# V' of a cross-attention block through device memory: all of it in fp32r rows, and context columns in another order

## The reference, cut to what matters

```
qh = layernorm(x) @ Wq ; kh = ctx @ Wk ; vh = ctx @ Wv        (16 heads of 64)
attn = softmax(causal(qh kh^T / 8))
x = x + concat_heads(attn vh) @ Wo + bo
h = layernorm(x); x = x + bitlinear(silu(bitlinear(h, w_gate)) * bitlinear(h, w_up), w_down)
```

## Time and profile before

| what | value |
|---|---|
| median of 3 runs | 697.3 us (696.67 to 698.23) |
| the profiled execution's own time | 696.44 us |
| its span, first to last instruction | 694.6 us |
| PE busy | 670.0 us, 96% of the span |
| DVE, ACT, POOL busy | 538.7, 488.2, 350.1 us |
| DMA | 63.04 MB moved, 91 GB/s over the span |
| mean granted PE clock, 1 being full speed | 0.990 |

### The profile page before, as it was taken

One profiled execution on the slowest core, in us unless ns is written; L12 is line 12 of the kernel. 1 busy time (PEld: TensorE's weight loads), 2 busy tenths in 40 slices (PEclk: granted clock), 3 DMA queues, 4 the chain that ended last, 5 costly groups with the idle time before them and its releaser, 6 DMA issues.

```text
span 694.6 us, 18984 instructions
## 1 busy us (share of the span) xinstructions
PE 670.0 (96%) x7235; PEld 450.7 (65%) x7266; DVE 538.7 (78%) x1398; ACT 488.2 (70%) x864; POOL 350.1 (50%) x357
## 2 busy tenths in 40 slices
PE   8999999999999999999999999999999999999963
PEld 5576766677666667666666767666676766667451
DVE  5667878777788777787877778787777887787976
ACT  5768767767866767876676787667678667768543
POOL 0536554554555555455455455546454554644541
PEclk9999999999999999999999999999999999999995
DMA  8023433333433434343333334343333433332421
GB/s 267 2 77 92 99 86 85 86 96 88 109 100 74 95 77 102 84 115 78 97 88 82 103 86 110 81 92 86 85 100 92 110 74 96 86 82 72 99 60 38
DMA packets 71834, 63.04 MB, mean 91 GB/s; under 512 B 43584, under 2 KB 47936, under 8 KB 71744
## 3 DMA queue, kind: packets, MB, share of 16 engines
q1 hardware_dynamic: 71744, 61.83, 36.4%
HBM read 15.91 MB, written 4.19 MB: 29 GB/s over the span
## 4 chain that ended last, share of the span: by engine, by line
PE 91%; DVE 3%; issue 2%; POOL 2%; DMA 1%; ACT 0%; POOLq 0%; SPq 0%; DVEq 0%
PE ps_up L460 8%; PE ps_up L344 7%; PE ps_a L485 7%; PE ps_b L571 6%; PE ps_up L333 5%; PE ps_up L334 4%; PE ps_up L335 4%; PE ps_kv L344 4%; PE ps_low L344 4%; PE ps_a L489 4%; PE ps_low L470 4%; PE ps_u L553 2%; PE ps_up L352 2%; PE ps_up L354 2%; PE ps_up L353 2%
## 5 line engine op out<-in xcount | busy, mean ns | idle before, releaser
L665 ACT ACTIVATE vp<-ps_up 128x512 f32<-128x512 f32 x61 | 36.4, 597 | 134.5 <-PE ps_up L344 134.5
L1192 POOL TENSOR_TENSOR prob_up<-prob_up,row_rec 128x512 f32<-128x512 f32 x62 | 63.8, 1051 | 125.3 <-DVE row_rec L975 125.3
L1178 POOL TENSOR_TENSOR hid_b<-hid,neg_round 128x512 bf16<-128x512 f32 x62 | 63.1, 1039 | 94.8 <-ACT hid L665 94.8
L1183 POOL TENSOR_TENSOR prob_up<-prob_up,row_max 128x1024 f32<-128x1024 f32 x31 | 59.3, 1913 | 61.0 <-DVE row_max L960 61.0
L1024 DVE SCALAR_TENSOR_TENSOR gated<-gated,ps_g 128x512 f32<-128x512 f32 x60 | 41.2, 687 | 54.3 <-ACT gated L749 53.3
L953 DVE SCALAR_TENSOR_TENSOR prob_up<-ps_up,rs,bias_up 128x512 f32<-128x512 f32 x62 | 43.7, 747 | 45.3 <-PE ps_up L460 45.3
L665 ACT ACTIVATE kp<-ps_up 128x512 f32<-128x512 f32 x124 | 71.0, 605 | 10.1 <-PE ps_up L335 7.5
L485 PEld LDWEIGHTS ps_a<-vp,prob_t 128*32 128x32 f32 x1984 | 55.3, 110 | 19.0 <-issue 17.9
L460 PE MATMUL ps_up<-kp,xt 128*32 128x256 f32 (+1 forms) x768 | 61.9, 454 | 0.0
L344 PE MATMUL ps_up<-n_w,ct 128*32 128x512 f32 x504 | 60.2, 593 | 0.9 <-DVE prob_up L953 0.9
L485 PE MATMUL ps_a<-vp,prob_t 128*32 128x128 f32 x1984 | 59.9, 273 | 0.8 <-ACT prob_t L665 0.8
(11 more groups left out here) (257 smaller groups left out, 1806.5 us busy)
## 6 DMA issues: line engine op xcount, KB each, us to landing
vp<-v_rows SPq DMA_DIRECT2D x496, 64.0 KB, 2.0
ct<-in_ctx_t SPq DMA_DIRECT2D x16, 256.0 KB, 2.9
x_res<-in_x SPq DMA_DIRECT2D x16, 256.0 KB, 2.8
xt<-in_x_t SPq DMA_DIRECT2D x16, 256.0 KB, 3.2
out<-x SPq DMA_DIRECT2D x32, 128.0 KB, 2.4
kp<-v_rows SPq DMA_DIRECT2D x16, 64.0 KB, 2.0
hid_t<-hid_b SPq DMA_TRANSPOSE x62, 2.9
kp<-in_wk SPq DMA_DIRECT2D x2, 256.0 KB, 4.0
```

The costliest lines, as they stand in the source:

```text
L665: copy = lambda dst, src, **kw: nc.scalar.activation(dst, src, ACT.Copy, **kw)
L1178: p.tensor_tensor(hid_b[:, c, :], hid[0][:, c, :], neg_round[:].broadcast_to([P, F]), ALU.add).then_inc(hb_ready, 1)
L1183: p.tensor_tensor(up, up, top[:, 0, :].rearrange("p (c h o) -> p c h o", c=1, o=1) .broadcast_to([P, 2, H, R]), ALU.subtract).then_inc(shi ...
L1192: p.tensor_tensor(up[:, half, :, :], up[:, half, :, :], rows(rec[:, 0, :], H, R), ALU.mult).then_inc(normed, 1)
```

## The change

1. **V' wholly by rows.** `v_tiles` is gone. `v_unit` makes eight units for a quad, four for each half (`jh`), each three products as in `v_row_unit`. `v_rows` has eight buffers in place of four. A quad's eight units are made in the period before its own.
2. **Through device memory.** `save_row` writes each unit to a scratch tensor `v_mem` in device memory (4 MB, two quads deep; 256 KB are written per unit); `load_v` reads the quad's whole V' back into `vp` with one 2 MB DMA, or two of 1 MB for the last quad. The 16 moves per quad are gone.
3. **Column order.** The context columns are stored as (half, key, sequence) in place of (half, sequence, key). The K' copies put them back: they read PSUM at a step of four elements and write in order. `sum_ctx` reads at that step too.
4. **Order of the fill.** Between the other work of a period PE places 16 units in the order `o0 o1 o2 o3 k0 k1 o4 k2 o5 k3 o6 k4 o7 k5 k6 k7` (o: V' of the next quad, k: K'), at the positions that the tiles and units had.
5. **N.** ACT writes `n_hi` straight from PSUM, DVE makes `n_lo` from PSUM and `n_hi`; `scores(0)` waits for all four `n_lo`.
6. **Small steps.** POOL makes `rstd2(n-1)` between the upper and the lower subtraction. `sum_ctx` comes after the inverted sums. In the ending several steps of PE, ACT, DVE and POOL change places, and so do PSUM banks.

```diff
-    in_ctx_t: .transpose(0, 5, 1, 3, 2, 4)
+    in_ctx_t: .transpose(0, 5, 1, 3, 4, 2)
-            def v_tiles(n, b, dst):
-                col = (n % 2 * 4 + 2) * P // 2 + b * R
-                for h4 in range(QB):
-                    t = mm(dst[h4 * R:(h4 + 1) * R, :], ct[n // 2 % 2][:, col:col + R], heads_of(n_w, h4), ...)
+            def v_unit(n, u, dst):
+                par, col = n // 2 % 2, (2 * (n % 2) + u // QB) * P
+                cols = slice(col, col + P)
+                hi, lo = heads_of(n_hi, u % QB), heads_of(n_lo, u % QB)
                 mm(dst, ct_hi[par][:, cols], hi, start=True, stop=False)
                 mm(dst, ct_lo[par][:, cols], hi, start=False, stop=False)
                 mm(dst, ct_hi[par][:, cols], lo, start=False, stop=True).then_inc(rows_ready, 1)
-            def move_rows(n, h4):
-                sp.wait_ge(rows_evac, QB * n + h4 + 1)
-                for b in range(QB):
-                    sp.dma_start(vp[...][h4 * R:(h4 + 1) * R, b, 0, :, :], v_rows[h4][b * R:(b + 1) * R, :, :])
+            def save_row(n, u):
+                jh, h4 = u // QB, u % QB
+                if n >= 2:
+                    sp.wait_ge(vp_loaded, 16 * (n - 1))
+                sp.wait_ge(rows_evac, V_UNITS * n + u + 1)
+                sp.dma_start(v_mem[n % 2, h4 * R:(h4 + 1) * R, :, jh, :], v_rows[u][...]).then_inc(rows_saved[u], 16)
+            def load_v(n):
+                if n and n < LAST:
+                    sp.wait_ge(attn_ready, n)
+                for u in range(V_UNITS):
+                    sp.wait_ge(rows_saved[u], 16 * (n + 1))
+                sp.dma_start(vp[last(n)]..., v_mem[n % 2]...).then_inc(vp_loaded, 16)
 SP, per period:  turn_hid(n-2)
-                 move_rows(n, 0..3), load_ctx, load_xt; store(n-2); x_res
+                 load_v(n); x_res; load_xt or load_ctx; save_row(n+1, 0..3); store(n-2); save_row(n+1, 4..7)
 PE, attend(n):
-                pe.wait_ge(v_evac, V_UNITS * n + V_UNITS)
-                for h4 in range(QB):
-                    pe.wait_ge(vp_moved[h4], 16 * QB * (n + 1))
+                pe.wait_ge(vp_loaded, 16 * (n + 1))          (vp_end for the last quad)
 ACT, take_k:
-                copy(kp[par][:, h, :], banks[bank])
+                copy(kp[par][:, h, :].rearrange("p (c b j) -> p c b j", b=QB, j=R),
+                     banks[bank].rearrange("p (c j b) -> p c b j", b=QB, j=R))
 ACT, take_row(n, u):
+                if n:
+                    act.wait_ge(rows_saved[u], 16 * n)
 DVE, beginning:
+            n_low(0); n_low(1)      (after the biases)
+            n_low(2); n_low(3)      (after unseen)
 DVE, per period:
-                sum_ctx before sum_rows
+                sum_ctx after invert_sums
 POOL, per period:
-                lower(n); rstd2(n - 1)
+                lower_upper(n); rstd2(n - 1); lower_lower(n)
 DVE, ending:
-            quantise_x(A - 1); sum_rows(A, 0)      ...  second_residual(A - 1); gate_hid(A, 0); gate_hid(A, 1)
+            sum_rows(A, 0); quantise_x(A - 1)      ...  gate_hid(A, 0); gate_hid(A, 1); second_residual(A - 1)
 ACT, ending:
-            take_probs(B, 0..2); round_hid(A - 1, 0..1)
+            round_hid(A - 1, 0..1); take_probs(B, 0..2)
```

More of the change, by code:

```diff
@@ L210, in build, with fills, evacuated @@
         makes_k = lambda n: live(n) and n // 2 + 1 < GROUPS
+        FILL = "o0 o1 o2 o3 k0 k1 o4 k2 o5 k3 o6 k4 o7 k5 k6 k7"
+        FIRST_FILL = [("v", 0, u) for u in range(V_UNITS)]
+        def fills(n):
+            own = FIRST_FILL if n == 0 else []
+            if makes_k(n):
+                return own + [("kv"[c == "o"], n + (c == "o"), int(u)) for c, u in (w for w in FILL.split())]
+            return own + [("v", n + 1, u) for u in range(V_UNITS) if live(n + 1)]
+        def evacuated(n, i):
+            kind, m, u = fills(n)[i]
+            return (k_evac, H + K_UNITS * m + u + 1) if kind == "k" else (rows_evac, V_UNITS * m + u + 1)
         PERIODS = range(QUADS - 2)
@@ L475, in attend @@
                 pe.wait_ge(pt_evac, 3 * n + 3)
-                pe.wait_ge(v_evac, V_UNITS * n + V_UNITS)
-                for h4 in range(QB):
-                    pe.wait_ge(vp_moved[h4], 16 * QB * (n + 1))
+                if n == LAST:
+                    pe.wait_ge(vp_end, 32)
+                else:
+                    pe.wait_ge(vp_loaded, 16 * (n + 1))
                 if n and n < LAST:
@@ L743, in take_hid @@
                 act.wait_ge(ht_ready, c + 1)
-                copy(flat(hid_t[1][:, c, :, :]), banks[3 - c], bias=-ROUND).then_inc(ht_evac, 1)
+                copy(flat(hid_t[1][:, c, :, :]), banks[1 + c], bias=-ROUND).then_inc(ht_evac, 1)
             def tanh(n, c):
@@ L755, in _ @@
             for n in PERIODS:
-                if n == 0:
-                    for k in range(4):
-                        round_n(k)
                 if live(n, 2):
@@ L906, in m_low, with n_low @@
                 low_part(m_lo[:, k % 2, half, :], banks[k], m_hi[:, k % 2, half, :], SCALE, m_lo_done)
+            def n_low(k):
+                dve.wait_ge(n_hi_done, k + 1)
+                half = slice(4 * (k // 2), 4 * (k // 2) + 4)
+                low_part(n_lo[:, k % 2, half, :], banks[N_BANK[k]], n_hi[:, k % 2, half, :], 1.0, n_lo_done)
             centre_wq(0)
@@ L1074, in _ @@
                     quantise_x(n - 1)
-                if makes_k(n) and n % 2 == 0:
-                    sum_ctx(n // 2 + 1)
                 if live(n):
@@ L1080, in _ @@
                     invert_sums(n)
+                if makes_k(n) and n % 2 == 0:
+                    sum_ctx(n // 2 + 1)
                 if live(n, 2):
@@ L1178, in lift_hid, with lower_upper @@
                     p.tensor_tensor(hid_b[:, c, :], hid[0][:, c, :], neg_round[:].broadcast_to([P, F]), ALU.add).then_inc(hb_ready, 1)
-            def lower(n):
-                up, low, top = prob_up[last(n)], prob_low[last(n)], row_max[last(n)]
+            def lower_upper(n):
+                up, top = prob_up[last(n)], row_max[last(n)]
                 pool.wait_ge(max_done, 2 * n + 1)
```

341 lines of the change are left out of this document (155 added, 186 removed).

## The result

The changed kernel takes 685.5 us (median, 684.81 to 686.25), the kernel before on the same chip 697.2: a ratio of 0.983, 95% interval 0.981 to 0.985. It is faster by 11.7 us. The time lies in the range of the prediction, but 6 us above its 679.5. The profiled execution took 686.25 us, its span is 684.5; it stands against the 696.44 of before, so the two profiles differ by 10.2 us where the medians differ by 11.7.

The account below looks back on a forecast made before the run. PE, busy 96% of the span, was taken as the bound. Periods 1 to 29 gave -19.4, period 0 +2.1, beginning +0.8, ending -1.3: -17.8 from 697.3 makes 679.5 us, range 676 to 691.

Parts of the forecast that it names:

- The mechanism: Periods: PE bounds the kernel, so a microsecond less PE work is a microsecond less period, until something PE needs is late.
- What PE itself needs: PE per period: four row units (2.76 us) replace four tiles (3.43), 0.67 less, giving 19.74 us.
- I take 0: First half of probabilities: ready at +14.3, PE asks at +14.5; wait taken as 0, bounds 0 and 0.3 per period.
- bank 3: PE's eighth unit: one of four places where PE is 0.2 to 0.5 us early or late.
- the rival of small waits: Four places in each period: PE waits 0.15 to 0.45 us in total, giving 684 to 692 us; chance 0.18.
- stepped read: DVE's `sum_ctx`: reading at a step stays 0.4 us; its move takes 0.33 off every second period and is covered.
- POOL's order: `rstd2` between POOL's subtractions: `xn` ends at about +9.3 against +9.50, 0.2 us won, not 0.7.
- Copies of K': ACT's evictions reading PSUM at a step of 16 bytes: 0.60 us each, bounds 0.60 and 1.02.
- the rival of half rate: ACT's K' copies at 1.02 us each: `xq_t` late by 0.66 per period, 698.6 us; chance 0.08.
- DMA: Transfers per period: 13.8 of 19.74 us, 70%, or 83% with dearer writes; no bound, `vp` landing 8 to 12 us after issue.
- The beginning: `scores(0)` waits for four `n_lo` and starts 0.8 us late; bounds 0 and 1.3.
- The ending: After the periods: earlier probabilities of quad A and earlier gate products, together 1.3 us less; bounds 0 and 4.1.

Follow-up runs that it names:

- e9_exp_later: `e6_three_waits` with ACT's lower exponential one eviction later, behind the fifth unit's: 680.2 us, ratio 0.976, mean period 19.75.
- e3_late_sum_last: The changed kernel with `sum_ctx` after the late residual (`add_late`) on DVE: 685.8 us, ratio 0.984, even period 19.91.
- e5_take3_first: The changed kernel with ACT evicting the fourth V' unit (bank 3) before the lower exponential: 685.1 us, ratio 0.983.
- e6_three_waits: The changed kernel with the moves of `e5_take3_first` and `e3_late_sum_last`, and POOL's lower subtraction held until `xn` is done: 685.8 us, ratio 0.984.
- e12_without_hold: `e9_exp_later` without the hold of POOL's lower subtraction: 684.3 us once, 687.1 three times, ratio 0.986, mean period 19.92.
- e1_no_transport: The changed kernel without saves and reads of V' except the first quads' and the last read: 684.8 us, ratio 0.984.
- e4_double_saves: The changed kernel with every V' unit written twice, the second time to an unread scratch tensor: 743.1 us, ratio 1.066.
- e2_pool_order_back: The changed kernel with POOL making both subtractions before `rstd2`, as before the change: 689.9 us, ratio 0.990.
- e10_plus_head: `e9_exp_later` with all four `n_lo` made ahead of the late sums in the beginning: 681.0 us, ratio 0.976.
- e11_one_read: `e10_plus_head` with one 2 MB read of the last quad's V' in place of two of 1 MB: 682.3 us, ratio 0.979.
- e8_all: `e6_three_waits` plus all four `n_lo` before the late sums and the save/read order of `e7_end_order`: 692.0 us, ratio 0.994.
- e7_end_order: The changed kernel with the last quad's first 1 MB read issued ahead of its last four saves: 691.1 us, ratio 0.992.

## Why the prediction was right, and where its size was off

**The mechanism held.** PE bounds the periods; less work on PE made them shorter. What PE itself needs came out as forecast: 19.75 measured in `e9_exp_later`, 19.74 forecast. The gain per period from PE's work alone is thus 20.39 - 19.75 = 0.64, against 0.67: the period of before was 20.39 in the mean, not the 20.41 that was read from an even one (the odd ones took 20.37), and with the 0.01 of the new period this makes 0.9 us of 29 periods.

**The step that failed is "I take 0".** The prediction put the first half of the probabilities at +14.3 and PE's asking at +14.5, called it the tightest place, and priced it at 0 with a bound of 0.3. It named bank 3 as 0.2 to spare. Both stop PE, by 0.05 to 0.14 and by 0.10. The mean period of 19.96 against the 19.75 of `e9_exp_later` is 0.21, 29 x 0.21 = 6.1 us. That is as much as the gap between 685.5 and 679.5, but partly by luck: in the profiles 7.6 us are missing, of which the waits are 6.1, the period read too long 0.9, the ending 1.0 and the beginning 0.3, less 0.5 of period 0. So the rival of small waits (0.15 to 0.45 per period, 684 to 692), given 0.18, is what happened. The forecast's own range, 676 to 684, missed; the range of 676 to 691 held the result because it took in this rival.

Two errors of reading stand behind it. The first is in the slack of 0.2. PE's asking was read from the chain, 327.06, whose pieces start when the piece before is done; the timeline of before has the same transposes start at 326.90:

```profile
326.90 0.60 PE L571 MATMUL ps_b<-id_sb,prob_up 128*128 128x128 f32 x4
```

That is +15.02, not +15.18, and so +14.38 now, not +14.5. (In `e9_exp_later`, where nothing holds them up, they start at 321.68, +14.35.) The half was ready at +14.36 for +14.3, and the 0.1 from release to start wasn't counted: no slack is left. The second error is a wait that was missed altogether. `prob_transposes(n, 0)` waits for `late_added` too, and `sum_ctx` stands ahead of it on DVE, so it isn't covered, as the prediction said it was. Besides, its stepped read didn't stay at 0.4: the median of its 16 instructions went from 0.42 to 0.51. `e3_late_sum_last` shows that wait's 0.10 in every second period.

**The waits are not a sum.** `e5_take3_first` took away the wait at bank 3 and won nothing; `e3_late_sum_last` won 0.10 in every second period and no more; `e6_three_waits` took away three and won nothing; `e9_exp_later` moved one more step of ACT and won 5.3 us; `e12_without_hold` took one back and its trace lost 0.16 per period. DVE to POOL, DVE to the late residual, and ACT's queue to `xq_t` all end within 0.3 us of when PE asks. PE waits for the last of them: by the traces the late residual sets 20.01 in the even periods, POOL's first half 19.91, ACT's queue 19.97 once POOL is held, and PE itself 19.75. So a move wins no more than the distance to the next. Each of the hold and the later exponential is shown to be needed; a kernel with both but with `sum_ctx` where the change has it wasn't run.

**The other terms.** POOL's order: 0.2 forecast, 0.14 measured. Copies of K': 0.60 as taken; the rival of half rate fell. The Trainium skill (SBUF — State Buffer, Door 1: The DMA port swizzle) has its warning of non-contiguous PSUM access for matmuls, and for ACT's reads at this step the rows show none of it. DMA: a share of 0.71 to 0.78 and reads that land 9.0 us after issue, as forecast (0.70, 8 to 12); `e1_no_transport` shows that it costs nothing and `e4_double_saves` where it would. The beginning: PE's wait and its cause were right, 1.1 for 0.8; the load of the first inputs alone moves this start by some 1.2 us between executions (DVE's first `n_lo` began at 20.76, 21.54 and 21.91 in three kernels with the same beginning up to there), so the 0.3 means nothing.

**The ending.** The first half of the step was right: quad A's attention came 23.2 us after its scores (628.54 to 651.76, by the timeline) where it took 25.0 (638.30 to 663.27), 1.7 sooner. DVE's gate products of that quad came earlier too, 37.8 us after the scores (666.31) for 39.0 (677.25). But the prediction took no wait of the last quad for its own rows: they are made in the ending itself, saved and read back, and PE stood still 3.1 us for them, so that quad B's attention came 30.6 after the scores of A, against 30.0 before (668.34). That is a new wait of the kind that the prediction looked for in the periods and not here, and it ate the ending's gain down to 0.3. The kernels that keep this order of saves and reads show it. From the start of scores(30) to the end, `e2_pool_order_back`, `e5_take3_first`, `e6_three_waits`, `e9_exp_later`, `e10_plus_head` and the changed kernel took 54.2, 54.8, 55.1, 55.1, 55.4 and 55.9 us, with 1.4, 1.9, 2.2, 2.3, 2.6 and 3.1 of wait: 52.8 besides the wait, each time. (`e1_no_transport` took 0.4 less, `e3_late_sum_last` and `e12_without_hold`, in whose endings the granted clock fell to half for some 8 us, 1.5 and 0.9 more.) Without the wait the ending would thus be some 3.4 us shorter than before, an estimate, where 1.3 was forecast. Why the wait differs so much among kernels with the same ending isn't known. A difference of up to 1.7 us between two of these kernels can be this wait alone. The moves of before, from SBUF to SBUF, had only one flight; this has two in a row, 2.0 for the last save and 9.2 for the read. A version that moves the last quad's rows in the old way wasn't tried.

## What to carry to other kernels

When a change takes work off an engine that is busy all the time, list every semaphore that the engine takes up in a period with its slack, from the program and not from the trace, and price each slack that is as small as the error of its own sum at half its bound, not at zero. Waits that end close together must be moved together; tried one by one, each can look worthless, and a gain of 1 us can also be hidden by the ending of the same execution. And look at the last round of a pipeline separately: a transport that is hidden in every period is bare in the last.

## What the runs showed of the hardware

- ACT reads PSUM at a step of 16 bytes as fast as in order: 0.60 us for 128x512, in 120 copies of the largest group.
- Writes of 256 KB in pieces of 2 KB beside reads of 2 MB saturated the DMA engines at 336 GB/s (share 1.03). In the ending, four saves that stood behind a 1 MB read in the queue landed 7.0 to 7.4 us after issue, not 2.0 to 2.5, and held up a second read by 6.
- Two `tensor_scalar` instructions of DVE beside POOL's subtraction took 1.32 us, alone 0.60, and one of 128x2 took 0.67, alone 0.17. The Trainium skill (SBUF — State Buffer, Who interferes with whom) says that the two share a pair of ports under a lock; the trace agrees. Holding POOL back for it paid only once ACT, which waits for POOL, had other work in the meantime.
- DVE's sum over 128x256 that reads SBUF at a step of four elements took 0.51 us, in order 0.42 (medians of 16).
- Behind the wait for the last read, the granted clock fell in some executions and not in others with waits as long. After 2.56 us of standing still (`e3_late_sum_last`), 2.79 (`e11_one_read`), 5.32 (`e8_all`) and 5.65 (`e7_end_order`) PE ran the next 64 products in 3.3 to 3.4 us, at a granted clock of 0.62 to 0.66 over the 4 to 5 us around them; after 2.61 (`e10_plus_head`) and 3.12 (the changed kernel) in 1.96, at the full clock.
